# Three places in an instruction order: the second group's high part ahead of silu, and two DVE pieces behind the second half scan

## The chip, the cores and the metric

One core of one Trainium2 chip (trn2). The metric is device time in microseconds (us) of one execution; the kernel before takes 2794.8 us, the median of 3 runs (2794.27 to 2800.88). The engines are called PE (TensorE), DVE (VectorE), ACT (ScalarE), POOL (GpSimd) and SP (SyncE, which here only issues DMAs).

## The reference, cut to what matters

A decoder layer over 32 batches of 256 tokens of width 256, in float32. Three parts, each followed by a residual and a layer norm:

```python
x = _layernorm(x + attn_ref(x, ...))          # a selective scan (Mamba): in-projection, causal conv of 3 taps, silu,
                                              # x_proj, softplus(dt), dA = exp(delta * A), dBu = delta * B * u,
                                              # carry = dA * carry + dBu in chunks of 64 tokens, y = sum(carry * C),
                                              # y * silu(gate), out-projection
x = _layernorm(x + xattn_ref(x, ctx, ctx))    # 16 heads of width 16, softmax over 256 keys
x = _layernorm(x + ffn_ref(x, w1, w3, w2))    # 8 experts, silu(x w1) * (x w3), w2
```

## The kernel before

The first two parts ("mixers") run in one software pipeline over the 32 batches and take most of the time; the experts follow as a block of their own and are not touched. Each engine has its own list of *pieces*, each with an offset. `run_steps` turns the list into an instruction order: a piece with offset o runs in slot o modulo 16 of step (batch + o // 16), and pieces of one slot run in the order in which they stand in the list. So one step of 16 slots is one period of the pipeline, and in each slot an engine works for several batches at different stages. An engine executes its instructions in that order, and each piece begins with the semaphore waits that it needs.

The pieces that matter, by engine:

- **Scan part.** For each of 16 tiles t, in two halves of 128x512: ACT makes `decay(t, 0)` and `decay(t, 1)` (L615, two exponentials each, into one of three PSUM banks `dA_ps`), POOL makes `dBu` (L515), DVE runs `scan(t, 0)` and `scan(t, 1)` (L799), and then `hC` (L812 on DVE, L525 on POOL) multiplies with C. A decay waits until its bank was read three half tiles before. PE sums the states (`state_sum`) into `y_ps`, DVE gates, PE does `out_proj` into `a_ps`, and `residual(0, ...)` on DVE (L831 add, L834 and L840 statistics) adds the input. ACT then normalises (`norm(0, ...)`). The bank `a_ps` is next written by a convolution, which waits for the residual's add.
- **Before the scans.** PE convolves (`conv(m)`), ACT evacuates (`conv_evac`, L549) and runs `silu`: a table load, silu of u, silu of the gate, a table load back (L566, L562, L569). PE's `x_proj` and `dt_proj` and ACT's `xp_evac` and `softplus` (L600) follow.
- **Attention.** PE makes the scores of a head, DVE takes the row maxima (`row_max`, L856). For each group of 4 heads PE transposes the maxima into `y_ps` (`max_transpose`, L1075), ACT evacuates their high part (`max_high`, L715), DVE the low part (`max_low`, L862), a DMA takes both out and another brings them back as rows; PE then makes the transposed scores, ACT the exponentials (L677), PE the products with v (`pv`), ACT evacuates (`oT_evac`), PE transposes back into `f_ps` (`head_transpose`, L1118) and DVE divides by the sums (`head_norm`: L876 reciprocal, L881 product). The bank `f_ps` is shared: `v_proj`, `dt_proj` of the second half, the gate projection, `pv` and `head_transpose` wait for its last reader.

Numbers of the offsets put `silu`, `decay(9, .)` and `max_high(1)` of three batches before into slot 9 of ACT, in this order: silu, decay(9, 0), max_high(1), decay(9, 1), and an exponential. On DVE, slots 0, 4, 8 and 12 hold `head_norm(0)` to `head_norm(3)` between `scan(t, 0)` and `scan(t, 1)` for t = 15, 3, 7, 11, and slot 5 holds `residual(0, ...)` between `scan(4, 0)` and `scan(4, 1)`; `row_max` closes each slot, with `max_low(1)` behind `row_max(8)` at the end of slot 9. PE has `conv(1)`, `head_transpose(1)` in slot 3, `out_proj` in slot 4, `pv(2)` and `conv(2)` in slot 5, `conv(3)` and `head_transpose(2)` in slot 7, the transpose of the first norm's output and `max_transpose(1)` in slot 8, `pv(3)`, `x_proj` and `state_sum(1)` in slot 9, `head_transpose(3)` in slot 11, the transposed scores, `v_proj`, the transpose of the normalised heads and `max_transpose(2)` in slot 12. `low` (L846) for k stands in slot 0 of DVE between the two scans, and the attention's out-projection on PE waits for it.

Of the kernel before, what the change touches and what calls it, by code (L numbers as in the profile page):

```python
# [23 lines left out]
HG = 4  # L24
NG = H // HG
# [14 lines left out]
NU = DI // CT  # L40
# [21 lines left out]
O_SCAN = 17  # L62
# [8 lines left out]
O_MT = 52  # L71
# [123 lines left out]
def mixers(nc, io, x2_dram, scratch, shared):  # L195
# [3 lines left out]
    with ExitStack() as ctx:  # L199
# [336 lines left out]
        def _(act):  # L536
# [41 lines left out]
            def later_gate_evac(half):  # L578
                def piece(b):
                    if b.back(1):  # L580
                        gate_evac(half)(b)
                return piece
# [37 lines left out]
            def norm(i, s_mv, s_steps, s_x):  # L620
                def piece(b):
                    act.wait_ge(s_mv, b.value(TT, TT))
                    nc.scalar.activation(rstd[:, i], mv[:, i, :, 1], ACT.Ln, bias=eps).then_inc(s_steps, 1)
                    act.wait_ge(s_steps, b.value(5, 1))
                    nc.scalar.activation(rstd[:, i], rstd[:, i], ACT.Exp, scale=-0.5).then_inc(s_steps, 1)
                    act.wait_ge(s_steps, b.value(5, 2))
                    nc.scalar.activation(nrstd[:, i], rstd[:, i], ACT.Copy, scale=-1.0).then_inc(s_steps, 1)
                    act.wait_ge(s_steps, b.value(5, 3))
                    for tt in range(TT):
                        nc.scalar.activation(shift[:, i, tt:tt + 1], mv[:, i, tt, 0:1], ACT.Identity,  # L630
                                             scale=nrstd[:, i, tt:tt + 1]).then_inc(s_steps, 1)
                    for tt in range(TT):
                        act.wait_ge(s_steps, b.value(5, 4 + tt))
                        nc.scalar.activation(xt[:, b.c % NX, tt], xt[:, b.c % NX, tt], ACT.Identity, bias=shift[:, i, tt:tt + 1],
                                             scale=rstd[:, i, tt:tt + 1]).then_inc(s_x, 1)
                return piece
# [69 lines left out]
            def max_high(gr):  # L706
                def piece(b):
                    act.wait_ge(s_mT_mm, b.value(NG, gr + 1))

                    if gr >= 2:  # L710
                        act.wait_ge(s_m_dram, b.value(NG * 16, 16 * (gr - 1)))
                    else:
                        if b.back(1):
                            act.wait_ge(s_m_dram, b.back(1).value(NG * 16, 16 * (NG + gr - 1)))
                    nc.scalar.activation(m_rows[:, gr % 2, 0], y_ps[0:HG * TT, L:], ACT.Copy,  # L715
                                         scale=-1.0).then_inc(s_m_hi, 1)
                return piece
# [11 lines left out]
            def max_load(gr):  # L729
# [7 lines left out]
            run_steps([  # L737
                (O_SP + 1, softplus),
                (O_V + 1, v_evac),
                (O_SILU, silu),  # L740
                *[(O_GATE + 4 * half + 2, later_gate_evac(half)) for half in range(2)],
                (O_SP + 2, first_gate),
# [3 lines left out]
                *[(O_MT + HG * gr + 2, max_store(gr)) for gr in range(NG)],  # L746
                *[(O_MT + HG * gr + 3, max_load(gr)) for gr in range(NG)],
                (O_XP + 1, xp_evac),
                *[(O_MT + HG * gr + 1, max_high(gr)) for gr in range(NG)],
                (O_N2, norm(1, s_mv2, s_ln2, s_x2)),  # L750
                *[(O_CONV + 4 * half + 3, conv_evac(half)) for half in range(2)],
                (O_ONT - 1, onT_evac),
# [11 lines left out]
        def _(dve):  # L764
# [22 lines left out]
            def scan(t, half):  # L787
                def piece(b):
                    n = b.value(NU, t)
                    dve.wait_ge(s_dA, 2 * n + half + 1)  # L790
                    dve.wait_ge(s_dBu, n + 1)
                    decays = dA[(2 * n + half) % NDA][:].rearrange("p q t -> p (q t)")
                    dst = h[:, n % NH, 2 * half:2 * half + 2].rearrange("p q t -> p (q t)")
                    if (t, half) not in HC_DVE:
                        if n >= NH:
                            dve.wait_ge(s_sum, (n - NH) // 4 + 1)
                    else:
                        dst = decays
                    nc.vector.tensor_tensor_scan(  # L799
                        dst, decays, dBu[:, n % NB, 2 * half:2 * half + 2].rearrange("p q t -> p (q t)"),  # L800
                        0.0, ALU.mult, ALU.add).then_inc(s_scan[half], 1)
                return piece

            def hC_piece(t, half):

                def piece(b):
                    n = b.value(NU, t)
                    state = dA[(2 * n + half) % NDA]
                    dve.wait_ge(s_scan[half], n + 1)
                    if n >= NH:  # L810
                        dve.wait_ge(s_sum, (n - NH) // 4 + 1)
                    nc.vector.tensor_tensor(  # L812
                        h[:, n % NH, 2 * half:2 * half + 2], state[:],
                        bc_r[:, b.par, 1, 2 * half:2 * half + 2], ALU.mult).then_inc(s_hC_v, 1)
                return piece
# [10 lines left out]
            def residual(i, s_mm, src_ps, s_r, s_st, s_mv, s_steps, s_in, per_batch):  # L826
                def piece(b):
                    r = xt[:, b.c % NX]
                    dve.wait_ge(s_mm, b.value(TT, TT))
                    dve.wait_ge(s_in, b.value(per_batch, per_batch))  # L830
                    nc.vector.tensor_tensor(r, src_ps[:], r, ALU.add).then_inc(s_r, 1)  # L831
                    dve.wait_ge(s_r, b.value(1, 1))
                    for tt in range(TT):
                        nc.vector.bn_stats(st[:, i, tt], r[:, tt]).then_inc(s_st, 1)  # L834
                    if b.back(1):
                        dve.wait_ge(s_steps, b.back(1).value(5, 5))
                    dve.wait_ge(s_st, b.value(TT, TT))
                    nc.vector.memset(pad, 0.0)
                    for tt in range(TT):
                        nc.vector.bn_aggr(mv[:, i, tt], st[:, i, tt]).then_inc(s_mv, 1)  # L840
                return piece

            def low(s_hi, s_lo):
                def piece(b):
                    dve.wait_ge(s_hi, b.value(1, 1))
                    nc.vector.tensor_tensor(parts[:, 1], a_ps[:], parts[:, 0].bitcast(F32),  # L846
                                            ALU.subtract).then_inc(s_lo, 1)
                return piece
# [18 lines left out]
            def head_norm(gr):  # L867
                def piece(b):
                    dve.wait_ge(s_on_mm, b.value(NG, gr + 1))
                    src = f_ps[:, 1, :].rearrange("p (a h i) -> p a h i", a=TT, h=HG)  # L870
                    if gr:
                        dve.wait_ge(s_on, b.value(NG, gr))
                    else:
                        if b.back(1):
                            dve.wait_ge(s_on, b.back(1).value(NG, NG))
                    nc.vector.reciprocal(rsum[:], src[:, :, :, DK]).then_inc(s_rsum, 1)  # L876
                    dve.wait_ge(s_rsum, b.value(NG, gr + 1))
                    if b.back(1):
                        dve.wait_ge(s_onT_mm, b.back(1).value(1, 1))
                    dst = on[:, :, HG * DK * gr:HG * DK * (gr + 1)].rearrange("p a (h i) -> p a h i", i=DK)  # L880
                    nc.vector.tensor_tensor(dst, src[:, :, :, 0:DK],  # L881
                                            rsum[:].unsqueeze(3).to_broadcast([P, TT, HG, DK]),
                                            ALU.mult).then_inc(s_on, 1)
                return piece
# [2 lines left out]
                *[(O_SCAN + t, scan(t, 0)) for t in range(NU)],  # L887
                (O_OF + 1, residual(1, s_of_mm, a_ps, s_r2, s_st2, s_mv2, s_ln2, s_x1, TT)),
                (O_K + 1, low(s_k_hi, s_k_lo)),
                (O_OUT + 1, residual(0, s_out_mm, a_ps, s_r1, s_st1, s_mv1, s_ln1, s_xtok, 16)),  # L890
                *[(O_ON + HG * gr + 1, head_norm(gr)) for gr in range(NG)],
                *[(O_SCAN + t, scan(t, 1)) for t in range(NU)],
                *[(O_SCAN + t, hC_piece(t, half)) for t, half in HC_DVE],
                *[(O_S + hd + 1, row_max(hd)) for hd in range(H)],
                *[(O_SCAN + 4 * m + 6, gating(m)) for m in range(ND)],
# [570 lines left out]
```

## Time and profile before

| | |
|---|---|
| device time, median of 3 runs | 2794.8 us (2794.27 to 2800.88) |
| the profiled execution | 2790.39 us, span 2788.5 us |
| mean granted clock of PE | 0.95 |
| busy: PE, DVE, ACT, POOL | 2425.0, 2148.2, 1840.4, 2008.2 us |
| mixers in full flow | from 284 to 2103 us of the span |

The first few batches fill the pipeline, the last ones drain it until about 2320 us, and the experts take the rest. In the trace a period can be told by the first table load of `silu` (L566), of which there is one for each batch; the text counts batches from 0 by these 32 loads.

### The profile page before, as it was taken

How to read it: one execution, taken by the hardware profiler on the slowest of the kernel's cores; microseconds unless marked ns; L12 is line 12 of the kernel's file. 1: busy time of each engine (PE TensorE's matmuls, PEld its weight loads, DVE VectorE, ACT ScalarE, POOL GpSimd, SP SyncE). 2: the span in 40 equal slices, each digit the busy share in tenths (PEclk: the TensorE clock that was granted, in tenths of full speed). 3: DMA queues.
4: the chain of work that ended last, by engine and by line, in shares of the span. 5: the costliest groups of instructions: out<-in, count | busy, mean ns of one | idle time of the engine just before them, and what ended most of it. 6: DMA issues, size and time to landing. Idle time of an engine off the chain costs nothing. (4 is left out here: it accounts for less than half of the span.)

```text
span 2788.5 us, 49586 instructions
## 1 busy us (share of the span) xinstructions
PE 2425.0 (87%) x14816; PEld 1668.8 (60%) x14816; DVE 2148.2 (77%) x3262; ACT 1840.4 (66%) x4007; POOL 2008.2 (72%) x1000
## 2 busy tenths in 40 slices
PE   5678888899888889888989889898897869999998
PEld 3356666666666666666666666666665545555554
DVE  2788999999999999999999999999999732322332
ACT  3667888888888888888888878888887541111111
POOL 4998999999999999999999999999999400000000
PEclk9888999999999999999999999999999879999999
DMA  4465666666666676666666666666666360343221
GB/s 145 116 141 150 155 163 168 160 161 158 158 158 159 165 166 169 158 165 166 164 168 162 165 161 163 174 166 162 172 161 154 86 181 12 92 129 93 78 79 31
DMA packets 319321, 399.63 MB, mean 143 GB/s; under 512 B 115697, under 2 KB 256241, under 8 KB 314962
## 3 DMA queue, kind: packets, MB, share of 16 engines
q1 hardware_dynamic: 303698, 384.91, 53.9%
q10 hardware_dynamic: 15360, 11.55, 1.5%
q8 instruction: 124, 2.03, 0.3%
q14 instruction: 139, 1.14, 0.2%
HBM read 300.86 MB, written 94.37 MB: 142 GB/s over the span
## 5 line engine op out<-in xcount | busy, mean ns | idle before, releaser
L515 POOL TENSOR_TENSOR arena<-arena 128x1024 f32<-128x1024 f32 x512 | 1208.6, 2364 | 77.5 <-DMA arena<-w_dram 67.1
L615 ACT ACTIVATE dA_ps<-arena,a_neg 128x256 f32<-128x256 f32 x2048 | 880.1, 465 | 253.4 <-DVE arena L812 110.8
L799 DVE TENSOR_TENSOR_SCAN arena<-dA_ps,arena 128x512 f32<-128x512 f32 x608 | 728.1, 1207 | 85.2 <-ACT dA_ps L615 75.4
L525 POOL TENSOR_TENSOR arena<-arena 128x512 f32<-128x512 f32 (+1 forms) x416 | 739.1, 1777 | 61.8 <-DVE arena L799 58.7
L799 DVE TENSOR_TENSOR_SCAN dA_ps<-dA_ps,arena 128x512 f32<-128x512 f32 x416 | 493.2, 1205 | 3.1 <-POOL arena L515 2.7
L906 PE MATMUL a_ps<-xT,w_conv 128*128 128x256 f32 x1536 | 367.0, 389 | 0.0
L856 DVE TENSOR_REDUCE mx<-s_ps 128x2 f32<-128x512 f32 x497 | 334.5, 673 | 24.0 <-PE s_ps L906 23.9
L677 ACT ACTIVATE probs<-st_ps 128x512 f32<-128x512 f32 x493 | 285.5, 579 | 54.2 <-PE st_ps L906 46.5
L906 PEld LDWEIGHTS a_ps<-xT,w_conv 128*128 128x128 f32 x1536 | 286.8, 193 | 53.3 <-issue 16.5
L906 PE MATMUL s_ps<-k_st,q_st 96*128 96x256 f32 x994 | 266.6, 351 | 51.9 <-DVE mx L856 39.4
L906 PE MATMUL y_ps<-arena,sel 128*32 128x256 f32 x4096 | 257.7, 394 | 50.5 <-DVE m_rows L862 27.1
L812 DVE TENSOR_TENSOR arena<-dA_ps,arena 128x512 f32<-128x512 f32 x416 | 275.0, 678 | 6.6
L906 PE MATMUL st_ps<-q_st,k_st 96*128 96x256 f32 x986 | 222.3, 308 | 45.2 <-ACT probs L677 35.0
L906 PEld LDWEIGHTS s_ps<-k_st,q_st 96*128 96x128 f32 x994 | 171.5, 200 | 96.2 <-issue 62.8
L906 PEld LDWEIGHTS st_ps<-q_st,k_st 96*128 96x128 f32 x986 | 158.2, 198 | 106.7 <-issue 83.5
L906 PEld LDWEIGHTS y_ps<-arena,sel 128*32 128x32 f32 x4096 | 128.4, 112 | 138.6 <-POOL arena L525 53.5
L1275 DVE TENSOR_TENSOR hT<-silu,u_ps 128x512 f32<-128x512 f32 x80 | 54.9, 686 | 193.7 <-PE u_ps L1346 160.7
L1248 ACT ACTIVATE silu<-g_ps 128x512 f32<-128x512 f32 (+1 forms) x96 | 56.5, 596 | 209.9 <-PE g_ps L1346 209.8
L906 PE MATMUL a_ps<-bias 2*128 2x512 f32 (+2 forms) x192 | 93.4, 487 | 110.2 <-DVE parts L846 39.7
L1346 PE MATMUL g_ps<-arena 128*128 128x512 f32 x384 | 181.7, 599 | 3.1 <-PEq L199 3.1
L906 PE MATMUL f_ps<-probs,v 128*32 128x256 f32 x2048 | 154.9, 425 | 0.8 <-ACT probs L677 0.7
L1346 PE MATMUL u_ps<-arena 128*128 128x512 f32 x320 | 150.4, 592 | 0.0
(112 smaller groups left out, 3268.0 us busy)
## 6 DMA issues: line engine op xcount, KB each, us to landing
arena<-delta_dram SPq DMA_DIRECT2D x512, 128.0 KB, 2.8
arena<-w_dram SPq DMA_DIRECT2D x512, 128.0 KB, 3.3
arena<-bc_dram SPq DMA_DIRECT2D x128, 256.0 KB, 4.5
q_st<-q_parts_dram SPq DMA_DIRECT2D x512, 64.0 KB
k_st<-k_parts_dram SPq DMA_DIRECT2D x512, 64.0 KB
w_dram<-u SPq DMA_DIRECT2D x32, 512.0 KB, 2.9
delta_dram<-delta SPq DMA_DIRECT2D x32, 512.0 KB, 3.8
k_parts_dram<-parts SPq DMA_DIRECT2D x32, 512.0 KB, 4.0
```

The source lines that it names most:

```text
L515: pool.tensor_tensor(dBu[:, n % NB], w_r[:, n // RP % 2, t % RP].unsqueeze(1).to_broadcast([P, QS, L]), bc_r[:, b.par, 0], ALU.mult).then_ ...
L525: pool.tensor_tensor(h[:, n % NH, states], h[:, n % NH, states], bc_r[:, b.par, 1, states], ALU.mult).then_inc(s_hC, 1)
L615: last = nc.scalar.activation(dA[n % NDA][:, q], delta_r[:, n // (2 * RP) % 2, t % RP], ACT.Exp, scale=a_neg[:, t, 2 * half + q:2 * half + ...
L677: nc.scalar.activation(probs[:, n % NPROB], scores_T_bank(n), ACT.Exp, scale=float(DK) ** -0.5).then_inc(s_exp, 1)
L799: nc.vector.tensor_tensor_scan(dst, decays, dBu[:, n % NB, 2 * half:2 * half + 2].rearrange("p q t -> p (q t)"), 0.0, ALU.mult, ALU.add).t ...
L812: nc.vector.tensor_tensor(h[:, n % NH, 2 * half:2 * half + 2], state[:], bc_r[:, b.par, 1, 2 * half:2 * half + 2], ALU.mult).then_inc(s_hC ...
L856: nc.vector.tensor_reduce(mx[:, hd], scores_bank(b.value(H, hd)), AX.X, ALU.max).then_inc(s_max, 1)
L906: return nc.tensor.matmul(out, lhsT, rhs, start=first, stop=last)
L1248: nc.scalar.activation(dst, g_ps[i % 2][first:last], ACT.Silu).then_inc(f_silu, 1)
L1275: nc.vector.tensor_tensor(hT[first:last, i // 2, HALF * (i % 2):HALF * (i % 2 + 1)], silu[first:last, i % 2], ups[first:last], ALU.mult).t ...
L1346: ins = nc.tensor.matmul(ps[i % 2][:], w13[:, b.par, k, col:col + P], x2T[:, b.par, k, cols], start=(k == 0), stop=(k == KD - 1))
```

## The change

In ACT's list `max_high(1)` moves from behind `decay(., 0)` to the head of slot 9, ahead of `silu`. In DVE's list the second half scans move ahead of `residual(0, ...)` and the four `head_norm` pieces. `low` for k and `residual(1, ...)` stay between the two halves. No instruction is added or removed, and no DMA is moved in its queue.

```diff
             run_steps([
                 (O_SP + 1, softplus),
                 (O_V + 1, v_evac),
+                (O_MT + HG + 1, max_high(1)),
                 (O_SILU, silu),
...
-                *[(O_MT + HG * gr + 1, max_high(gr)) for gr in range(NG)],
+                *[(O_MT + HG * gr + 1, max_high(gr)) for gr in range(NG) if gr != 1],
...
                 (O_K + 1, low(s_k_hi, s_k_lo)),
+                *[(O_SCAN + t, scan(t, 1)) for t in range(NU)],
                 (O_OUT + 1, residual(0, s_out_mm, a_ps, s_r1, s_st1, s_mv1, s_ln1, s_xtok, 16)),
                 *[(O_ON + HG * gr + 1, head_norm(gr)) for gr in range(NG)],
-                *[(O_SCAN + t, scan(t, 1)) for t in range(NU)],
```

## Rows read from the trace of the kernel before

**Rows 1.** Busy time by engine in the stretch of full flow (windows; PE, PEld, DVE, ACT, POOL, clock).

```profile
284.00:2103.00 1819.00, 1611.22 (x11255) 1169.22 (x11255) 1682.94 (x2458) 1475.48 (x3267) 1684.93 (x838) 0.97 0.65 163
```

**Rows 2.** Waits of DVE in total, times, and the longest (us).

```profile
DVE m_rows L862 <- ACT m_rows L715: 62.6, 31, 2.1
...
DVE x_tok L831 <- PE a_ps L906: 40.6, 42, 7.4
...
DVE rsum L876 <- PE f_ps L1118: 37.1, 34, 9.0
```

**Rows 3.** Timeline of ACT: start, duration; the silu block and what follows it.

```profile
284.25 1.28 ACT L566 ACT_TABLE_LOAD   x1
...
1232.86 1.28 ACT L566 ACT_TABLE_LOAD   x1
...
1300.84 1.28 ACT L566 ACT_TABLE_LOAD   x1
...
1305.45 0.87 ACT L615 ACTIVATE dA_ps<-arena,a_neg 128x256 f32<-128x256 f32 x2
1306.27 0.25 ACT L715 ACTIVATE m_rows<-y_ps 8x128 fp32r<-8x128 f32 x1
...
1367.38 1.28 ACT L566 ACT_TABLE_LOAD   x1
...
1433.93 1.28 ACT L566 ACT_TABLE_LOAD   x1
...
2103.19 1.28 ACT L566 ACT_TABLE_LOAD   x1
```

**Rows 4.** Timeline of DVE in slots 9 to 12.

```profile
1306.55 0.28 DVE L862 SCALAR_TENSOR_TENSOR m_rows<-y_ps,m_rows 8x128 fp32r<-8x128 f32 x1 [2.13 <-ACT m_rows L715]
...
1315.32 1.22 DVE L799 TENSOR_TENSOR_SCAN arena<-dA_ps,arena 128x512 f32<-128x512 f32 x1 [0.56 <-ACT dA_ps L615]
...
1316.67 0.29 DVE L881 TENSOR_TENSOR on<-f_ps,rsum 128x128 f32<-128x128 f32 x1
```

**Rows 5.** Timeline of DVE in slots 4, 5 and 8.

```profile
1347.16 0.21 DVE L876 RECIPROCAL rsum<-f_ps 128x8 f32<-128x8 f32 x1 [0.43 <-PE f_ps L1118]
...
1351.84 0.69 DVE L831 TENSOR_TENSOR x_tok<-a_ps,x_tok 128x512 f32<-128x512 f32 x1 [0.55 <-PE a_ps L906]
...
1366.86 0.66 DVE L856 TENSOR_REDUCE mx<-s_ps 128x2 f32<-128x512 f32 x1
```

**Rows 6.** Timeline of PE from slot 0 to slot 8.

```profile
1331.63 0.46 PE L906 MATMUL a_ps<-bias 2*128 2x512 f32 x1 [1.33 <-DVE parts L846]
...
1361.80 2.76 PE L906 MATMUL a_ps<-xT,w_conv 128*128 128x256 f32 x12
...
1367.58 0.37 PE L1075 MATMUL y_ps<-ident,mx 128*8 128x128 f32 x1 [1.61 <-DVE mx L856]
```

**Rows 7.** Timeline of ACT in slot 8, ahead of the next silu block.

```profile
1364.60 0.60 ACT L549 ACTIVATE u<-a_ps 128x512 f32<-128x512 f32 x1 [0.29 <-PE a_ps L906]
1365.49 0.88 ACT L615 ACTIVATE dA_ps<-arena,a_neg 128x256 f32<-128x256 f32 x2 [0.29 <-DVE arena L799]
...
1366.78 0.59 ACT L657 ACTIVATE x1T<-a_ps 128x512 f32<-128x512 f32 x1
```

**Rows 8.** Timeline of PE in slots 12 and 13.

```profile
1317.15 0.49 PE L906 MATMUL f_ps<-bias 4*128 4x512 f32 x1
1317.57 2.00 PE L906 MATMUL f_ps<-w_v,ctxT 128*128 128x256 f32 x8
...
1323.00 0.47 PE L906 MATMUL s_ps<-k_st,q_st 96*128 96x256 f32 x2 [1.36 <-DVE mx L856]
```

**Rows 9.** Two like stretches of two batches (windows; the clock stands third from the end).

```profile
1263.00:1270.00 7.00, 6.36 (x33) 4.17 (x34) 6.80 (x14) 3.98 (x11) 7.00 (x4) 0.76 0.75 154
1331.00:1338.00 7.00, 6.37 (x40) 4.54 (x41) 6.80 (x14) 4.18 (x10) 7.00 (x5) 1.00 0.78 148
```

**Rows 10.** Timeline of PE in slot 12, one batch later.

```profile
1384.10 3.26 PE L906 MATMUL f_ps<-w_v,ctxT 128*128 128x256 f32 x8
```

## The prediction

> **What bounds the kernel now.** I first read the page's busy times, then the windows over full flow. DVE and POOL are both at work for 1683 to 1685 of 1819 us, 93%, and ACT and PE for less [rows 1]. So no engine is simply full; the question is where the last 7% of DVE goes. The table of waits names three causes of DVE idleness near the change: `max_low` waits for ACT's `max_high` (62.6 us in 31 waits), `residual` waits for PE (40.6 in 42), `head_norm` waits for PE (37.1 in 34) [rows 2]. These are the edits' targets, 140 us in all, but a wait that goes may only move. For that I followed one period in the timelines, the one whose silu block begins at 1300.84 and ends with the next at 1367.38, 66.54 us later [rows 3]. From 284.25 to 2103.19 there are 27 periods, a mean of 67.37 [rows 3].
>
> The period closes through three engines in turn. (1) In DVE's slot 0, `low` for k releases PE at 1331.63, and PE then has no idle row until `max_transpose(1)` at 1367.58 [rows 6]. On that unbroken run lies `conv(3)`, 1361.80 to 1364.56. (2) ACT's `conv_evac` waits for it and starts at 1364.60, then comes `decay(8, 1)`, which waits another 0.29 for a DVE scan, the exponential, the evacuation of x1T at 1366.78, and the silu block at 1367.38 [rows 3, 7]. From there ACT is full through softplus to `decay(11, .)`, and DVE's `scan(11, 0)` waits 0.56 for that at 1315.32 in the period shown [rows 4]. (3) From that scan DVE works on without a break to `low` for k. So between slots 4 and 8 the DVE is only 0.29 us behind what PE permits, and between slots 9 and 11 ACT decides.
>
> **The move of max_high(1).** What it removes: DVE's 2.13 us before `max_low(1)` at 1306.55 [rows 4]. ACT ran `decay(9, 0)` at 1305.45 for 0.87 and `max_high(1)` at 1306.27 [rows 3]. With the maxima early, `max_low(1)` can follow `row_max(8)` at once, but the next DVE piece is `scan(9, 0)`, which needs `decay(9, 0)`, done at 1306.32, against 1306.83 where it had to wait for `max_low`. So of 2.13 us at most some 0.5 is free at that place, the rest turns into a wait of the scan for ACT; and that 0.5 is then spent in the wait before `scan(11, 0)`, since ACT's softplus decides there. What it adds: 0.15 us to silu (`max_high` takes 0.25 and overlaps its neighbour by 0.1, as the spacing in [rows 3] shows), given back behind `decay(9, 0)`, where it no longer stands. Net on the path through softplus: nothing. PE's `state_sum(1)`, which waited for `max_low`, can start earlier; PE is not late in slots 9 to 11, so I take nothing for it.
>
> The danger is that `max_high(1)` waits for `max_transpose(1)` at the head of ACT's queue, with silu, x_proj and all decays behind it. In the order before, the transpose runs from 1367.58 to 1367.95 and is released by `row_max(7)`, which starts at 1366.86 [rows 5, 6]; ACT would be free at 1367.26. So with DVE as late as it is now, silu would move from 1367.38 to 1367.95 + 0.25 = 1368.20, a loss of 0.82, or 0.67 after the 0.15 that is given back. The Trainium skill ("TensorE: Matmul & The Clock Gate", section "Architectural detail", on queue depths) calls ACT's and DVE's queues strictly first in, first out: nothing passes a waiting `max_high`. The trace agrees, in that DVE's scan stands behind the 2.13 us wait of `max_low`; by that rule the move alone would be a loss. Whether it is one depends on the second edit.
>
> **The second half scans ahead of residual and head_norm.** In slot 4 `scan(3, 1)` can run while `head_norm(1)` would wait (0.43 in this period), in slot 5 `scan(4, 1)` while the residual waits for out_proj (0.55) [rows 5]. Both decays are made by then, ACT having run ahead. A second half scan takes 1.13 from start to start, more than either wait, so both go: DVE is 0.98 ahead in slots 5 to 8. The residual itself hardly moves: `scan(4, 0)` now ends 0.55 + 0.43 ahead of out_proj, and with 1.13 of `scan(4, 1)` behind it the residual starts 0.15 later than before; the first norm and the next conv into `a_ps` have more slack than that. `row_max(7)` then ends near 1366.5, the transpose at 1367.95 − 0.98 = 1366.97. ACT: `conv_evac` cannot move (PE), `decay(8, 1)` loses its 0.29 wait, or 0.39 if the next activation starts 0.50 after conv_evac as usual. ACT is then ready for `max_high(1)` at about 1366.9 to 1367.0, just when it is there. Softplus and all that follows come 0.29 to 0.39 earlier; I take 0.33, near the middle. The other 0.65 of DVE's lead becomes a longer wait before `scan(9, 0)`.
>
> In about 22 of the 29 periods of full flow `head_norm(1)` waits, as here (most of the 34 waits of [rows 2]); in the other 7 that wait is missing, the lead is only 0.55, ACT is held some 0.4 by the transpose, and gain and loss cancel. 22 x 0.33 = 7.3 us. In the first and last batches the residual waits longer, up to 7.4 us; 42 waits minus some 28 of 0.55 leave 25 us in 14 waits [rows 2], but a scan hides 1.13 of one at most, and I count two of them, 2 us. Sum: −9.3 us. The profiled execution took 2790.4, so it would take 2781.1; the median of the runs is 4.4 higher, so 2794.8 − 9.3 = 2785.5.
>
> `head_norm(0)` and `(2)` cost nothing: their readers `pv(1)` and `pv(3)` come over 1 us later. `head_norm(3)` is another matter. It ended at 1316.96 [rows 4] and PE began `v_proj` into the same bank `f_ps` at 1317.15 [rows 8]. Behind `scan(11, 1)` it ends 1.13 later, at 1318.09, so PE gets a new wait of 0.98. Behind it stand v_proj, the transpose of the heads, `max_transpose(2)`, scores and `pv(0)`; PE next waits 1.36 for DVE at 1323.00 [rows 8], which takes it up with 0.38 left. I cost it at nothing. That it is hidden is borne out by the period from 1367.38: PE's `v_proj` took 3.26 there instead of 2.00 [rows 8, 10], yet the period is 66.55 [rows 3]. But with both, 1.26 + 0.98 = 2.24, it is 0.9 too late.
>
> **The clock.** The periods differ by PE's granted clock. The stretch 30 to 37 us behind the silu block ran at 0.76 in one period and at 1.00 in the next [rows 9]: part of it was at 1.2 GHz instead of 2.4, behind the 1.33 us wait for `low`. The first of these took 67.98, the second 66.54, so one fall on PE's unbroken run costs 1.44 [rows 3]. By the mean of 67.37, (67.37 − 66.54) / 1.44 = 58% of the 27 periods, or 16, pay it. The change leaves the wait before `low`, but moves the period's length, and so where a fall lands. I leave the number as it is and put both ends into the range: none gives −23, all give +16. The Trainium skill ("TensorE: Matmul & The Clock Gate", section "The HAM clock gate") says that the slow clock is the default and activity lifts it; the new wait of 0.98 before v_proj is, by this, an invitation to another fall.
>
> **Rivals.**
> - *The lead is spent elsewhere.* PE binds from slot 0 to 7; if `decay(8, 1)` or the exponential behind it also hangs on PE, the 0.33 is not there and DVE merely waits for `decay(9, 0)` instead of `max_high(1)`. For: the slack is but 0.29. Against: the idle row of 0.29 is DVE's. Time: 2790 to 2798.
> - *v_proj behind head_norm(3), with a slow clock.* If the clock falls there in half of 28 periods, 14 x 0.9 = 13 us are lost against 9.3 won: 2798. In all of them 25 − 9 = +16: 2811. It decides from a third of the periods on.
> - *max_high(1) holds silu.* Slower: if DVE's lead at `row_max(7)` is under about 0.5, ACT stands for the transpose. With no lead at all 0.67 x 28 = +19: 2814. Against it: the lead of 0.98 by the rows above.
> - *Falls of the clock move off the unbroken run.* Up to −23 more: 2762 to 2779.
>
> **How the numbers follow.** Forecast, 2779 to 2792: 0.38. Lead spent: 0.22. v_proj: 0.16, of which half is slower than by 0.3%. max_high holds silu: 0.12. Clock better: 0.12. A change of 0.3% (8.4 us: under 2786.4 or over 2803.2) is about what a measurement of this kernel tells from none. Faster: 0.32 of the forecast's 0.38 and the 0.12 of the clock, 0.44. Slower: 0.12 + 0.08 and some clock falls on top, 0.22. Same: 0.34. The range takes in half of the clock's better case and the smaller half of the slower ones: 2768 to 2806.
>
> **What would show it.** Right: L862's wait for L715 gone; in its place a wait of `scan(9, 0)` for L615 near 2.5 us; no wait at L876 in slot 4 nor at L831 in slot 5; ACT's silu block 0.1 to 0.2 earlier against conv(3); undisturbed periods near 66.2; PE waiting about 1 us for L881 before v_proj. Wrong: an ACT wait at L715 for PE L1075 just ahead of the table load; periods above 67 with DVE waiting in slot 13 for scores or `max_high(2)`; or another number of falls of the clock than 16.

## The result, and the profile after

The kernel with the change takes 2801.15 us (median of 20 runs, 2794.21 to 2810.51), the kernel before 2794.66 us (20 runs, 2783.77 to 2800.88), a ratio of 1.0025 [1.0013, 1.0037]. That is 6.5 us slower, where 2785.5 was forecast. It is within the range given and within the 0.3% that was called no change, but its interval excludes a gain. The profiled execution took 2806.49 us (span 2804.7) against 2790.39: 16.1 us apart, where the medians are 6.5 apart. So the two traces show the mechanism, but overstate the size of the loss.

Windows of the profile after, over full flow, in the columns of [rows 1]; the stretch is 17 us longer, at the same mean clock:

```profile
286.00:2122.00 1836.00, 1614.87 (x11255) 1171.15 (x11255) 1674.14 (x2458) 1470.25 (x3266) 1682.60 (x838) 0.97 0.63 161
```

Waits of the profile after: total, times, longest. All line numbers behind L600 are one higher than before.

```profile
DVE arena L800 <- ACT dA_ps L615: 163.1, 72, 42.1
POOL arena L515 <- DMA arena<-w_dram: 108.4, 34, 11.0
ACT v L642 <- PE f_ps L907: 84.5, 31, 3.6
DVE mx L857 <- PE s_ps L907: 45.5, 40, 2.2
PE f_ps L907 <- DVE on L882: 28.7, 30, 1.9
DVE x_tok L832 <- PE a_ps L907: 22.8, 14, 7.4
DVE rsum L877 <- PE f_ps L1119: 20.4, 8, 8.8
```

Against [rows 2]: the wait of `max_low` for `max_high` is gone from the list, that of the residual fell from 42 times to 14, that of `head_norm` from 34 to 8. So each edit took away all or much of the wait at which it aimed. In their place stand more waiting before the scans (75.4 us in 40 waits before) and four other rows: PE for `head_norm` ahead of `v_proj` (not in the list before), ACT for v (30.4 before), DVE for the scores (23.9 in 25), and POOL for the transfer of w (67.1 in 39).

ACT's timeline at the silu block, to be read beside [rows 3, 7]:

```profile
1304.33 0.59 ACT L657 ACTIVATE x1T<-a_ps 128x512 f32<-128x512 f32 x1
1304.80 0.25 ACT L715 ACTIVATE m_rows<-y_ps 8x128 fp32r<-8x128 f32 x1
1305.07 1.28 ACT L566 ACT_TABLE_LOAD   x1
...
1322.66 0.58 ACT L677 ACTIVATE probs<-st_ps 128x512 f32<-128x512 f32 x1
...
1326.36 0.60 ACT L642 ACTIVATE v<-f_ps 128x512 f32<-128x512 f32 x1 [3.12 <-PE f_ps L907]
```

`max_high(1)` finds its maxima ready and holds nothing. 18 us after the table load begins, ACT stands for v. DVE's timeline of the same period, to be read beside [rows 4]:

```profile
1307.56 0.27 DVE L863 SCALAR_TENSOR_TENSOR m_rows<-y_ps,m_rows 8x128 fp32r<-8x128 f32 x1
...
1310.59 1.22 DVE L800 TENSOR_TENSOR_SCAN arena<-dA_ps,arena 128x512 f32<-128x512 f32 x1 [2.76 <-ACT dA_ps L615]
...
1319.40 2.34 DVE L800 TENSOR_TENSOR_SCAN arena<-dA_ps,arena 128x512 f32<-128x512 f32 x2 [0.79 <-ACT dA_ps L615]
1321.87 0.29 DVE L882 TENSOR_TENSOR on<-f_ps,rsum 128x128 f32<-128x128 f32 x1
...
1327.15 0.69 DVE L857 TENSOR_REDUCE mx<-s_ps 128x2 f32<-128x512 f32 x1 [0.82 <-PE s_ps L907]
```

`max_low(1)` no longer waits; `scan(9, 0)` waits 2.76 instead. Behind the pair `scan(11, 0)`, `scan(11, 1)` comes `head_norm(3)`, and 5 us on DVE stands 0.82 for the scores. What lies between is in PE's timeline (beside [rows 8]):

```profile
1320.82 0.47 PE L907 MATMUL st_ps<-q_st,k_st 96*128 96x256 f32 x2 [1.14 <-ACT probs L677]
1322.30 0.61 PE L907 MATMUL f_ps<-bias 4*128 4x512 f32 x1 [1.01 <-DVE on L882]
1322.85 3.48 PE L907 MATMUL f_ps<-w_v,ctxT 128*128 128x256 f32 x8
...
1326.63 0.48 PE L907 MATMUL s_ps<-k_st,q_st 96*128 96x256 f32 x2
```

PE waits 1.14 for an exponential, as it did before, and right behind that 1.01 for `head_norm(3)`, which is new. Then `v_proj` takes 3.48 instead of 2.00: the clock has fallen, as the window over it shows (0.66):

```profile
1322.00:1327.00 5.00, 4.70 (x17) 3.66 (x18) 4.30 (x6) 1.88 (x5) 5.00 (x4) 0.66 0.22 86
```

SP's queue in the same stretch, and POOL, which waits at its end:

```profile
1326.41 0.33 SPq L404 DMA_DIRECT2D ctxT<-in_ctxT  x1
1326.97 0.37 SPq L412 DMA_DIRECT2D q_parts_dram<-parts  x1
1327.50 2.33 SPq L392 DMA_DIRECT2D arena<-delta_dram  x4
1329.87 1.81 SPq L392 DMA_DIRECT2D arena<-w_dram  x4
```
```profile
1335.75 2.37 POOL L515 TENSOR_TENSOR arena<-arena 128x1024 f32<-128x1024 f32 x1 [2.85 <-DMA arena<-w_dram]
```

The load of the next context may only start when `v_proj` has read the old one; `replicate(0)`, which brings delta and w for the scans of tile 0, stands behind it. Before, that load was issued at 1319.64, 18.8 us behind its silu block, and POOL waited 0.40 at 1329.16; now it is issued 21.3 behind it, and POOL waits 2.85.

One of PE's own waits has moved too. Before, PE stood 1.61 for `row_max(7)` ahead of `max_transpose(1)` [rows 6]; now it stands 0.35 there, and 1.39 for silu's output just behind, ahead of `x_proj`:

```profile
1304.27 0.27 PE L1076 MATMUL y_ps<-ident,mx 128*8 128x128 f32 x1 [0.35 <-DVE mx L857]
...
1307.47 0.89 PE L907 MATMUL a_ps<-u,w_x 128*96 128x256 f32 x3 [1.39 <-ACT u L566]
```

**The periods.** Each of the profiled executions has 27 periods of full flow. For each I noted where PE's granted clock fell to half (1.2 GHz instead of 2.4). There are four places, told by their distance from the first table load of silu: within 1.5 us of it; near 12 us; at 17 to 19 us, on `v_proj`; and at 31 to 33 us, on PE's unbroken run to conv(3).

```
                        falls near 1 / 12 / 17-19 / 31-33   period without a fall   mean
before                     14 /  0 / 10 / 12                    66.54                67.37
after                       0 /  5 / 22 / 0                     none                 68.01
```

In both traces each fall comes within 2 us of the end of a PE wait of more than 1 us. At the first place that is the wait for `row_max(7)` (1.6, before), near 12 us the wait for softplus (1.3, after), on `v_proj` the 1.14 for the exponential, in after together with the 1.01, and on the unbroken run the 1.33 for `low`. Not every such wait brings a fall.

In the after trace a period with the fall on `v_proj` takes 68.28 on average (22 of them). The other 5, each with a fall near 12 us, take 66.8 (the shortest 66.03). In 8 of the 22 the clock stays low twice as long as in the rest; they take 68.79, the others 67.99. Before, the 12 periods with a fall on the unbroken run cost most (67.97 to 68.33). A fall on `v_proj` cost anything from nothing ([rows 8, 10] are such a pair, 66.54 against 66.55) to 1.5: the eight periods with it and none on the unbroken run take 67.06 on average, against 66.58 for the seven without any fall. The falls near 1 us cost nothing that shows.

### The profile page after: what moved, and what is told of

Its sections match the earlier page's. It is cut to its first block and busy times, and to the rows that moved or that the text cites. A ratio compares the mean times of both kernels' runs of the same rounds, so it can differ in the third digit from the quotient of the medians.

```text
span 2804.7 us, 49586 instructions
## 1 busy us (share of the span) xinstructions
PE 2436.9 (87%) x14816; PEld 1676.9 (60%) x14816; DVE 2139.1 (76%) x3262; ACT 1835.2 (65%) x4007; POOL 2006.4 (72%) x1000
## 3 DMA queue, kind: packets, MB, share of 16 engines
q14 instruction: 139, 1.14, 0.2%
## 5 line engine op out<-in xcount | busy, mean ns | idle before, releaser
L515 POOL TENSOR_TENSOR arena<-arena 128x1024 f32<-128x1024 f32 x512 | 1207.8, 2363 | 108.4 <-DMA arena<-w_dram 108.4
L907 PEld LDWEIGHTS y_ps<-arena,sel 128*32 128x32 f32 x4096 | 122.7, 112 | 114.6 <-POOL arena L525 24.1
L1365 PE MATMUL d_ps<-arena,hT 128*128 128x256 f32 x640 | 145.9, 383 | 0.0
```

The source lines that it names most:

```text
L515: pool.tensor_tensor(dBu[:, n % NB], w_r[:, n // RP % 2, t % RP].unsqueeze(1).to_broadcast([P, QS, L]), bc_r[:, b.par, 0], ALU.mult).then_ ...
L907: return nc.tensor.matmul(out, lhsT, rhs, start=first, stop=last)
L1365: nc.tensor.matmul(d_ps[(2 * t + i) % ND_PS][:, 0:D], hT[:, k, tokens], w2[:, b.par, k], start=(k == 0), stop=False)
```

## The experiments

All ratios are to the kernel before in the same call, with 95% intervals. In the diffs, "before" and "after" name the kernel that is edited.

**Each edit alone.** First after's ACT order with before's DVE order, and the reverse:

```diff
 # before, ACT
+                (O_MT + HG + 1, max_high(1)),
                 (O_SILU, silu),
...
-                *[(O_MT + HG * gr + 1, max_high(gr)) for gr in range(NG)],
+                *[(O_MT + HG * gr + 1, max_high(gr)) for gr in range(NG) if gr != 1],
```

> The kernel before with max_high(1) alone put ahead of silu. By the prediction's rival, ACT stands for max_transpose(1) with no DVE lead to cover it: +0.67 us in each of 28 periods, 19 us slower (2814), with an ACT wait at max_high just ahead of the table load. Other view (this wait only takes the place of ACT's wait for the scan): no more than 3 us either way.

2818.96 us, 1.0083 [1.0064, 1.0103]. ACT's timeline:

```profile
1310.92 0.59 ACT L657 ACTIVATE x1T<-a_ps 128x512 f32<-128x512 f32 x1
1312.04 0.27 ACT L715 ACTIVATE m_rows<-y_ps 8x128 fp32r<-8x128 f32 x1 [0.53 <-PE y_ps L1076]
1312.33 1.28 ACT L566 ACT_TABLE_LOAD   x1
```

`max_high(1)` waits 0.53 for the transposition and silu stands behind it. The periods whose only fall is the one on the unbroken run average 68.68 here and 67.98 in before: +0.70, for 0.67 in the prediction. Alone, this edit costs what the third rival said of it without a lead of DVE: +21 us between the medians (2818.96 against 2797.57), for +19.

```diff
 # before, DVE
+                *[(O_SCAN + t, scan(t, 1)) for t in range(NU)],
                 (O_OUT + 1, residual(0, s_out_mm, a_ps, s_r1, s_st1, s_mv1, s_ln1, s_xtok, 16)),
                 *[(O_ON + HG * gr + 1, head_norm(gr)) for gr in range(NG)],
-                *[(O_SCAN + t, scan(t, 1)) for t in range(NU)],
```

> The kernel before with the five DVE pieces alone moved; max_high(1) stays behind decay(9, 0). Theory: max_high(1) brings nothing by itself, so this is as slow as the whole change, 2800 +- 4, with max_low's wait of 2.1 us back. Rival (max_high ahead of silu is what costs): faster than the kernel before by 5 us or more.

2799.17 us, 1.0011 [0.9997, 1.0026]: the DVE edit alone does not pay either. `max_low` still waits for `max_high`, longer than before:

```profile
DVE m_rows L862 <- ACT m_rows L715: 80.9, 31, 3.0
```

20 of its 27 periods have the fall on `v_proj`.

**head_norm(3) apart from the rest.** After with it back between the scans, and before with it alone behind them:

```diff
 # after, DVE
                 (O_K + 1, low(s_k_hi, s_k_lo)),
+                (O_ON + HG * 3 + 1, head_norm(3)),
                 *[(O_SCAN + t, scan(t, 1)) for t in range(NU)],
...
-                *[(O_ON + HG * gr + 1, head_norm(gr)) for gr in range(NG)],
+                *[(O_ON + HG * gr + 1, head_norm(gr)) for gr in range(NG - 1)],
```

> The changed kernel with head_norm(3) alone put back between scan(11, 0) and scan(11, 1); everything else stays changed. Theory (v_proj held): PE's wait of 1.0 us for head_norm's product before v_proj is gone, the slow clock no longer falls on v_proj in most periods, and the time is the forecast one, about 9 us under the kernel before (2785). Rival (the clock falls follow the period's length, or max_high(1) ahead of silu is the cost): it stays at or above the kernel before, 2795 to 2803.

2797.3 us, 1.0003 [0.9992, 1.0014]. It takes away the loss but shows no gain, and the gain is the other half of the forecast; the theory's 2785 is a miss. Undisturbed periods are indeed 66.15. But the clock now falls near 12 us in 14 periods, where before had none, and still 12 times on the unbroken run. Windows: the former place, the latter place in two periods with and without a fall.

```profile
1170.00:1174.00 4.00, 3.90 (x10) 2.87 (x11) 3.11 (x5) 3.97 (x8) 3.42 (x3) 0.59 0.87 197
1188.00:1195.00 7.00, 5.66 (x33) 3.62 (x31) 6.79 (x14) 4.55 (x12) 5.92 (x4) 0.76 0.69 137
...
852.00:859.00 7.00, 6.24 (x40) 4.54 (x41) 6.80 (x15) 4.51 (x12) 7.00 (x4) 1.00 0.76 156
```

Periods with the first fall alone average 66.76, with the second alone 67.59, with both 68.22. So 14 x 0.6 = 8.4 us are lost near 12 us, and 27 x 0.39 = 10.5 us won; the mean period is 67.30, against 67.37 before. The other 7 periods of e3 have a fall on `v_proj` and take 66.84, a price like that in before. This sum holds for the 27 periods of one execution: outside them the profiled run of e3 takes 977.6 us and that of before 971.4.

```diff
 # before, DVE
-                *[(O_ON + HG * gr + 1, head_norm(gr)) for gr in range(NG)],
+                *[(O_ON + HG * gr + 1, head_norm(gr)) for gr in range(NG - 1)],
                 *[(O_SCAN + t, scan(t, 1)) for t in range(NU)],
+                (O_ON + HG * 3 + 1, head_norm(3)),
```

> The kernel before with head_norm(3) alone put behind scan(11, 1). Theory (v_proj held): all of the loss and none of the gain, some 13 to 17 us over the kernel before (2808 to 2812), with the wait of 1.0 us before v_proj and DVE's waits for the scores behind it. Rival (the loss is elsewhere): within 3 us of the kernel before.

2816.84 us, 1.0074 [1.0058, 1.0089], above the 2808 to 2812 of the theory: moved alone, `head_norm(3)` costs 0.74%, the largest effect of any part besides `max_high`. Within the whole change it costs 0.22% (1.0025 against 1.0003). In both pairs the move takes the falls at 31 to 33 us away (12 in before and in e3, 0 here and in after) and makes those on `v_proj` many and dear (17 here, 22 in after). What differs is the place near 12 us: the move adds 6 falls there to before and takes 9 from e3's 14. At 0.6 each that would be 9 us of the 14 between the two effects. This is worked out from one execution each, and not tested.

**Without max_high(1)'s move.** Before, with residual and head_norm(0) to (2) behind `scan(t, 1)`:

```diff
 # before, DVE
-                (O_OUT + 1, residual(0, s_out_mm, a_ps, s_r1, s_st1, s_mv1, s_ln1, s_xtok, 16)),
-                *[(O_ON + HG * gr + 1, head_norm(gr)) for gr in range(NG)],
+                (O_ON + HG * 3 + 1, head_norm(3)),
                 *[(O_SCAN + t, scan(t, 1)) for t in range(NU)],
+                (O_OUT + 1, residual(0, s_out_mm, a_ps, s_r1, s_st1, s_mv1, s_ln1, s_xtok, 16)),
+                *[(O_ON + HG * gr + 1, head_norm(gr)) for gr in range(NG - 1)],
```

> The kernel before with residual and head_norm(0) to (2) moved, head_norm(3) and max_high(1) where they were. Theory (max_high(1) nets nothing once DVE leads): as the changed kernel with head_norm(3) between its scans, 2797 +- 3, undisturbed periods of 66.2. Rival (max_high ahead of silu is a cost of its own): under 2792.

2792.16 us (the edge between theory and rival), 0.9995 [0.9981, 1.001], against 1.0003 [0.9992, 1.0014] with `max_high(1)` moved as well; undisturbed periods 66.16 and 66.15. The intervals overlap, so no net effect of that move shows, and the 0.39 us come from the DVE order alone, as the prediction's sum had it.

**Filling PE's waits.** If a fall comes from PE's wait, matmuls of no use in the wait should take it away. Four, of 128x256 f32 each, into a free part of `y_ps`:

```diff
 # before (and e3)
+            def fill(n):
+                def piece(b):
+                    bank_y.wait_read(pe)
+                    for _ in range(n):
+                        mm(y_ps[:, 0:L], ident[:], w_q[:, 0], True, True)
+                return piece
...
+                (O_S, fill(4)),
                 *[(O_OF, attn_out(tt)) for tt in range(TT)],
```

They are extra work, and no output uses them. In before, ahead of the wait for `low`:

> The kernel before, with four matmuls of 128x256 into the free bank y_ps in every step of slot 0, where PE waits 1.3 us for low of k; their result is read by nobody. Theory (a fall of PE's clock on the unbroken run costs 1.44 us, and the wait is what brings it): the falls near 32 us behind the silu block (12 of 27 periods) go and with them up to 17 us: 2778 to 2785. Rival (the falls come from the place in time, whatever PE does in this wait, and cost elsewhere if not here): within 4 us of the kernel before, or slower by the work added.

2785.8 us, 0.9964 [0.995, 0.9978]. No fall on the unbroken run is left (12 before), but 8 have come near 12 us, and an undisturbed period takes 66.76 instead of 66.54, the fills being longer than the wait. The same on e3:

> The same four matmuls in slot 0 of the changed kernel with head_norm(3) between its scans. Theory: undisturbed periods near 66.2 in place of 68.2, so 0.3 us in each of 28 periods under the kernel before with the same matmuls, 10 us: 2768 to 2776. Rival (the gain of 0.33 us is eaten by other falls, those near 12 us behind the silu block): no faster than the kernel before with the matmuls.

2772.73 us, 0.992 [0.9899, 0.9941], as its theory said. And in after, `(O_S + 12, fill(4))` ahead of `v_proj`:

> The changed kernel with four such matmuls ahead of v_proj, where PE waits 1.0 us for head_norm(3); head_norm(3) stays behind scan(11, 1) and the wait stays too. Theory (the wait of 1.0 alone is hidden, only together with a slow clock it is too long): the falls on v_proj become rare, most periods are 66.2 to 67, and the time is 2785 to 2793. Rival (the wait itself costs, by the load of ctx and the stores behind it in SP's queue): no less than 2798.

2793.38 us, 0.9993 [0.9977, 1.0009]: not one fall on `v_proj` in 27 periods, nor near 32 (9 near 12), but periods of 67.25. PE's timeline says why (fills, then v_proj's bias):

```profile
1180.98 1.89 PE L907 MATMUL y_ps<-w_q,ident 128*128 128x256 f32 x8
1182.80 0.50 PE L907 MATMUL f_ps<-bias 4*128 4x512 f32 x1
```

Four fills take 1.89 us (each matmul of f32 runs as two), more than the wait of 1.01; two would take 0.94. So `(O_S + 12, fill(2))`:

> The changed kernel with two matmuls of 128x256 ahead of v_proj, not four: the four lasted 1.8 us there, 0.8 more than the wait for head_norm(3) that they fill, these last 0.9. Theory (wait alone hidden, slow clock behind it not): no falls on v_proj, and now the time of the kernel with head_norm(3) between its scans or better, 2786 to 2793, under the 2793.4 of the four. Rival (the wait of 1.0 us costs by itself, through SP's queue): 2793 or more.

2787.59 us, 0.9974 [0.996, 0.9988], where after itself is 1.0025. Falls on `v_proj` go from 22 to 4 (7 come back on the unbroken run), the mean period from 68.01 to 67.22. The same instruction order, with the wait for `head_norm(3)` filled, is 0.5% faster. The size alone does not show that this was the loss, for fills help in before too (e16 below), and the fill at 12 alone was not run there. But within this run the 7 periods without a fall take 66.66 and the 4 with one on `v_proj` 68.11, and all have the late `head_norm(3)`: the late piece is cheap until the clock falls behind it.

**Both waits filled by two.** On e3, at 12 ahead of the transposed scores and at 0:

```diff
 # e3, PE
+                (O_S + 12, fill(2)),
                 *[(O_E + hd, scores_T(hd)) for hd in range(H)],
...
+                (O_S, fill(2)),
                 *[(O_OF, attn_out(tt)) for tt in range(TT)],
```

> The changed kernel with head_norm(3) between its scans, and two matmuls (0.9 us) in each of two waits of PE: in slot 0 for low of k (1.3 us), in slot 12 for the exponential (1.15 us). Theory: as the four matmuls in slot 0 (2772.7), less 0.2 us in each period for the shorter fill and less the falls near 17 us: 2764 to 2770. Rival (two are not enough to hold the clock): falls near 32 us come back, 2780 or more.

2771.26 us, 0.9922 [0.9902, 0.9943], just above its 2764 to 2770, with no fall left but 13 near 12 us, and a clock of 0.99:

```profile
284.00:2082.00 1798.00, 1628.26 (x11476) 1182.58 (x11476) 1672.19 (x2458) 1473.83 (x3269) 1686.36 (x838) 0.99 0.65 165
```

Its control is the same fills in before:

> The kernel before with two matmuls in slots 0 and 12 each. Beside it stands the kernel with head_norm(3) between its scans and the same matmuls, 0.9922 of the kernel before. Theory (the gain of 0.33 us in a period is there and the falls took it back): this one is 0.3 to 0.5% slower than that, 2780 to 2786. Rival (the moves bring nothing): the same 2771.

2776.65 us, 0.9931 [0.9917, 0.9945], below the 2780 to 2786 of the theory. So nearly all of e10's gain is the fills', and the 0.1% between the two lies inside both intervals. Undisturbed periods are 66.54 against 66.13, but e16 has 3 falls near 12 us and e10 13.

**SP's queue.** `replicate(0)` issued ahead of the context's load:

```diff
 # after, SP
+                (O_REP, replicate(0)),
                 (O_K - 2, load_ctx),
...
-                (O_REP + 1, replicate(0)),
```

> The changed kernel with the first load of replicated delta and w (replicate(0)) put ahead of load_ctx in SP's order. load_ctx waits for v_proj, so whatever holds v_proj holds replicate(0) too, and POOL waits about 3 us for w in each period. Theory (DVE's wait for the scores decides, POOL's wait only in part): POOL's wait for w falls to under 1 us, the time by 2 to 6 us: 2795 to 2799. Rival (SP's queue carries the whole loss): 2785 or less.

2822.84 us, 1.0107 [1.0085, 1.0128], a miss. POOL's wait for w did not go (130.3 us in 31), it moved to 46.5 us behind silu, and PE got waits for the context:

```profile
PEld a_ps L907 <- DMA ctxT<-in_ctxT: 19.7, 21, 4.5
PE a_ps L907 <- DMA ctxT<-in_ctxT: 14.1, 13, 3.9
```

It decides nothing, since it adds a delay of its own. A second buffer for the context takes SP's wait for the last `v_proj` away without moving a DMA (`k_proj` and `v_proj` read `ctxT[:, b.par]`):

```diff
 # after
-        ctxT = sb("ctxT", [P, KD, L])
+        ctxT = sb("ctxT", [P, 2, KD, L])
...
-                wait_all(sp, (s_k_mm, KD, b.back(1), KD), (s_v_mm, TT, b.back(1), TT))
-                sp.dma_start(ctxT[:], src).then_inc(s_ctxT, 16)
+                wait_all(sp, (s_k_mm, KD, b.back(1), KD), (s_v_mm, TT, b.back(2), TT))
+                sp.dma_start(ctxT[:, b.par], src).then_inc(s_ctxT, 16)
```

> The changed kernel with two buffers for ctx, so that load_ctx in SP's queue waits for v_proj of two batches before and never for the present one; v_proj itself is as late as in the changed kernel. Theory (SP's queue passes the delay of v_proj to POOL's w, and DVE's waits for the scores are the other part): POOL's wait for w falls from 108 us to the 67 of the kernel before or less, DVE's wait for the scores stays, and 3 to 6 us come back: 2795 to 2798. Rival 1 (all of the loss goes through SP): 2788 or less. Rival 2 (none): 2801.

2783.18 us, 0.9964 [0.9948, 0.9981]. Waits:

```profile
ACT v L642 <- PE f_ps L907: 75.8, 31, 3.6
DVE mx L857 <- PE s_ps L907: 40.2, 33, 2.2
POOL arena L515 <- DMA arena<-w_dram: 20.6, 13, 12.6
```

POOL's wait for w falls from 108.4 us to 20.6, ACT's and DVE's stay. A period with the fall on `v_proj` (17) takes 67.45 against 66.11 of the others. In 11 of the 17 the clock is low for the usual time, and these take 67.04: 0.93 more, where the like periods of after take 67.99. The other 10 periods have a fall near 12 us, and here it costs nothing. The time is below the theory's 2795, in the range of the rival that puts the whole loss on SP's queue. The control is the buffer in before:

> The kernel before with two buffers for ctx. Theory (SP's wait for v_proj costs only where v_proj is late): v_proj is on time here but for the periods with a slow clock on it, POOL waits 67 us for w in all and is hardly late, so within 4 us of the kernel before, 2791 to 2795. Rival (the buffers help as such): 2785 or less, as much as they gave the changed kernel against the kernel before.

2777.07 us, 0.9927 [0.9909, 0.9944], where the theory had 2791 to 2795: it gains no less there. The change with the buffer on both sides is 0.9964 against 0.9927, some 0.4% slower, no less than without it. So SP's queue is a loss of its own in either kernel, and taking it away does not bring the change level. It does carry a part of what a fall on `v_proj` costs: with the buffer that price goes from 0.5 to 0.1 in before's order, and from about 1.9 to 0.9 in after's (periods of 67.99 and 67.04 against 66.1). In e13 the periods lock; ACT's timeline gives 66.55 and 66.54 between these:

```profile
1022.32 1.28 ACT L566 ACT_TABLE_LOAD   x1
...
1088.87 1.28 ACT L566 ACT_TABLE_LOAD   x1
...
1155.41 1.28 ACT L566 ACT_TABLE_LOAD   x1
```

Only 4 of its 27 periods pay a fall on the unbroken run (12 before), which is most of what its periods gain. Its 11 on `v_proj` cost next to nothing (66.64 against 66.56).

**Combinations.** The buffer with `fill(2)` at 12 in after; the buffer with both `fill(2)` on e3; the buffer on e3; the buffer with both `fill(2)` in before:

> The changed kernel with both remedies: two ctx buffers, and two matmuls ahead of v_proj. head_norm(3) still holds v_proj for 1.0 us. Theory (clock and SP's queue are the whole loss): faster than with either, most periods 66.0 to 66.2, 2768 to 2778. Rival (both remedies meet the same loss): as the better of the two, 2783.

> head_norm(3) between its scans, two matmuls in slots 0 and 12, and two ctx buffers; the rest as changed. Theory: v_proj is not held, so the buffers add little to the 2771 of the matmuls alone: 2766 to 2772. Rival: under 2762.

> The changed kernel with head_norm(3) between its scans, and two ctx buffers, no matmuls. The kernel before with two ctx buffers took 0.9927, in periods of 66.55 with only 4 costly falls in 27. Theory: undisturbed periods of 66.2; if the falls stay as rare, 9 us faster than it, 2768; if the other length brings more falls, up to 12 us slower than that. Rival: the two are equal whatever the falls.

> The kernel before with both remedies, two ctx buffers and two matmuls in slots 0 and 12. The kernel with the moves and both remedies took 0.9863. Theory: 8 to 14 us slower than that, 2767 to 2773. Rival (the moves bring nothing): 2759.

```
e15  after, buffer, one fill      2778.08   0.9933 [0.9914, 0.9952]   falls 8 / 9 / 6
e14  e3, buffer, both fills       2759.21   0.9863 [0.9841, 0.9884]   falls 12 / 0 / 0
e17  e3, buffer                   2788.98   0.9976 [0.9963, 0.9989]   falls 18 / 6 / 18
e18  before, buffer, both fills   2769.49   0.9910 [0.9897, 0.9924]   falls 2 / 0 / 0
```

e14 is the fastest kernel of the study, 1.37% under before and faster than the 2766 to 2772 of its theory. (The three numbers behind "falls" are those near 12 us, on `v_proj` and on the unbroken run; e18 has 10 more near 1 us, the others none.) Against its control e18 the new DVE order gains 0.5%, and the timelines of ACT, of e14 and then of e18, have periods of 66.13 and 66.54:

```profile
1012.48 1.28 ACT L566 ACT_TABLE_LOAD   x1
...
1078.61 1.28 ACT L566 ACT_TABLE_LOAD   x1
```
```profile
1084.17 1.28 ACT L566 ACT_TABLE_LOAD   x1
...
1150.71 1.28 ACT L566 ACT_TABLE_LOAD   x1
```

Without the fills the sign turns: e17 is 0.5% slower than e13, with 18 falls on the unbroken run against 4.

## Why the prediction was wrong

- **The waits.** Right, each near its size. `max_low`'s wait is gone; `scan(9, 0)` waits 2.76 (forecast near 2.5); slot 4 doesn't wait, slot 5 still 0.23 in the same period (forecast none); PE waits 1.01 before `v_proj` (forecast 0.98).
- **max_high(1).** Right as far as measured: no net effect shows (e6 beside e3), without DVE's lead it costs 0.70 a period, for 0.67 in the prediction (e1, +0.83%), and with the lead it is just in time (1304.80, then the table load at 1305.07). The wait of ACT's in-order queue is where the Trainium skill's rule from the prediction ("TensorE: Matmul & The Clock Gate", "Architectural detail") holds: e1 shows silu behind the waiting `max_high`.
- **"I take 0.33"** a period from the DVE order. Right where nothing disturbs: 66.54 became 66.15 in e3, 66.13 in e14, 0.39 to 0.41 a period, or 0.4 x 27 = 11 us. e14 against e18 is 10 us in the medians, but 6.3 us in the 27 periods of the two traces, e14 having 12 falls near 12 us and e18 2. The sum also counts the periods as 27, 28 and 29 in turn; the rows have 27.
- **"head_norm(3) is another matter ... I cost it at nothing."** The step that failed. The sum took the new wait of 0.98 as covered by the 1.36 behind it, and the slow `v_proj` of 1.26 as covered by the same 1.36. It said that both together are 0.9 too late, and left that to a rival with 0.16. They come together in 22 of 27 periods of the trace. The price is also more than 0.9: 67.99 in the 14 periods where the clock is low for the usual time, against about 66.1 undisturbed in this order (e15: 66.14 on average, e11: 66.12 at least), and 68.79 in the 8 where it is low for twice as long. The 0.9 was right for what goes over PE: with SP's queue freed it is 0.93 (e12). The rival's worst case, all periods, was 2811; the trace of after is near it, and the median of 2801 between its two. That the falls are what costs is shown by e3, where head_norm(3) is back and the loss gone, and within e11: 68.11 with the fall, 66.66 without one.
- **"I leave the number [of falls] as it is."** The second step that failed, and the reason why e3, free of the first, still gains nothing. Falls on the unbroken run were 12 in before (16 came from dividing the whole excess of the mean by 1.44, as if no other fall cost anything), and did not stay: 0 in after, 12 in e3, 18 in e17. The prediction spoke of one place for a fall with a price; there are four. Each of the seven kernels with before's DVE order at `row_max(7)` (before, e1, e4, e7, e13, e16, e18) has 4 or more falls near 1 us, behind PE's wait of 1.6, where they are free. None of the others has any, for the lead of DVE shortened that wait (to 0.35 to 0.76 in the periods looked at). Near 12 us, where before has none, after has 5 and e3 14, at some 0.6 each in e3. The prediction counted DVE's lead as a gain for ACT and did not ask what PE's shorter wait does to the clock.
- **What it did not look at.** SP's queue: `load_ctx` waits for `v_proj`, and `replicate(0)` for POOL stands behind it. It raised POOL's wait from 67.1 to 108.4 us and about doubles the price of a fall on `v_proj` (e12 against after). It does not explain why the change loses to before, since with it freed in both the change is still 0.4% slower (e12 and e13).

**Left open.** Why a fall lands behind one long wait of PE and not behind another, and so why the parts' costs don't add, no run settles; no run holds the wait near 1 us or fills the one near 12. The counts are of one execution for each kernel, and the two profiled ones are further apart than the medians. That e13 has few costly falls because its periods are even is argued from the even spacing, and not tested; in e17 the same buffer goes with 18. Also open: why a fall near 12 us costs 0.5 to 0.6 in e3, e14 and e17 and nothing in e12 and e15, where `head_norm(3)` is late and the buffer doubled.

## What to carry to other kernels

A piece moved behind its neighbour gives every engine that reads its buffer a new wait; a wait of 1 us on PE must be priced with the slow clock behind it, not with the row's normal duration, and followed into the DMA queue that waits for the same event. A gain in the undisturbed period is only worth what the falls of the clock leave of it: count the falls by place and price, in both kernels, and compare changes with the waits filled. Where PE waits for about 1 us in a periodic kernel, fill the wait with matmuls, no longer than the wait: here that was worth 0.7%, a second buffer for a late-read operand 0.7%, the two together 0.9% (e18), and the DVE order without `head_norm(3)` 0.5% more on top of both.

## What the runs showed of the hardware

- PE's granted clock fell to half behind waits of only 1.1 to 1.7 us. All 36 falls in the full flow of before and all 27 of after come within 2 us of the end of a wait of more than 1 us. On `v_proj` in after, where it fell in 22 of 27 periods, there are two, 1.14 and 1.01. The Trainium skill ("TensorE: Matmul & The Clock Gate", "The HAM clock gate") has the slow clock as the default that activity lifts. The fills agree with it, taking falls on `v_proj` from 22 to 4 (e11) or 0 (e9) and those of the unbroken run from 12 to 0 (e7), though other places then get some (8 near 12 us in e7).
- The same change of the clock has a price by its place. It is 1.44 us on the unbroken run (e3: 67.59 against 66.15) and nothing near 1 us. Near 12 us it is 0.6 in e3 and nothing in e12. On `v_proj` it is 0.5 in before, 0.1 with a second buffer (e13), 1.9 or more where `v_proj` is late (after), and 0.9 there with the second buffer (e12).
- A matmul of 128x256 f32 takes 0.47 us at the full clock and stands in the trace as two instructions (e9: 1.89 for four, x8).
